# Half of the last layer norms moved from the attention's logits stage into the convolutions' logits stages, in a four-layer graph network

## The reference

```python
h = relu(_layernorm(x)); x = x + L0(h, edge_attr, ...)   # GINE: gather, sum, MLP, batch norm
h = relu(_layernorm(x)); x = x + L1(h, ...)              # two GATv2 convolutions, 4 heads
h = relu(_layernorm(x)); x = x + L2(h, ...)              # GAT with a small MLP
h = relu(_layernorm(x)); x = x + L3(h, edge_index)       # x + 0.5 * mean over the edges
```

## Time and profile before

| | us |
|---|---|
| median of 3 runs (range) | 4635.77 (4630.58 to 4641.23) |
| the profiled execution, its own time | 4636.25 |
| its span | 4634.5 |
| conv_logits of convolution 0, start to the next stage's start | 1549.5 to 2075.8 |
| conv_logits of convolution 1, first gathers to its last logit | 2437.8 to 2965.8 |
| gat_logits, start to the next stage's start | 3389.3 to 3714.7 |

### The profile page before, as it was taken

The page is one execution under the profiler, slowest core; times in us unless marked ns, Lnnn a source line. Parts: engine busy times, 40 slices in busy tenths (PEclk is TensorE's granted clock), DMA queues, the critical chain, the costliest instruction groups (busy, mean ns, idle before and its releaser), DMA issues. The chain is left out here.

```text
span 4634.5 us, 66260 instructions
## 1 busy us (share of the span) xinstructions
PE 3307.0 (71%) x15560; PEld 1990.1 (43%) x15560; DVE 3210.8 (69%) x10235; ACT 2604.3 (56%) x7608; POOL 2915.7 (63%) x2865
## 2 busy tenths in 40 slices
PE   2544288688888699985987999678856559973332
PEld 2444133477777334333663343245522235553331
DVE  2322299688888578876876888679978868863332
ACT  2322299588888577763774777446667725530000
POOL 6777677488887677756877875135577400037776
PEclk7766599899999899997998999889978879975555
DMA  8433388567776466656984545299979957653331
GB/s 327 117 98 87 120 282 279 179 239 243 238 243 216 152 213 209 215 171 199 327 269 135 166 157 163 79 311 334 328 257 346 325 143 230 225 174 98 98 96 53
DMA packets 549485, 942.99 MB, mean 203 GB/s; under 512 B 86253, under 2 KB 170248, under 8 KB 547204
## 3 DMA queue, kind: packets, MB, share of 16 engines
q1 hardware_dynamic: 481252, 800.20, 51.4%
q0 software_dynamic: 65856, 113.13, 9.2%
q10 hardware_dynamic: 2016, 25.69, 1.3%
HBM read 563.37 MB, written 381.14 MB: 204 GB/s over the span
## 5 line engine op out<-in xcount | busy, mean ns | idle before, releaser
L1163 DVE TENSOR_TENSOR conv_logits_leaky<-conv_logits_z,conv_logits_sloped 128x512 f32<-128x512 f32 x784 | 516.8, 687 | 111.7 <-ACT conv_logits_sloped L1097 103.1
L1097 ACT ACTIVATE conv_logits_sloped<-conv_logits_z 128x512 f32<-128x512 f32 x784 | 459.4, 596 | 176.3 <-PE conv_logits_z L1059 121.2
L1438 PE MATMUL conv_aggregate_part<-conv_aggregate_weighed,conv_wlc 128*128 128x512 f32 x784 | 360.1, 603 | 38.9 <-DVE conv_aggregate_weighed L1520 38.9
L1059 PE MATMUL conv_logits_z<-conv_logits_hdT,conv_logits_wsum 128*128 128x512 f32 x784 | 367.2, 612 | 15.1 <-DVE conv_logits_leaky L1163 13.1
L1066 PE MATMUL conv_logits_z<-conv_diffT,conv_logits_wl 128*128 128x512 f32 x784 | 352.9, 593 | 0.0
L748 PE MATMUL node_chain_o<-node_chain_ident,node_chain_biasT 128*128 128x128 f32 x784 | 220.5, 281 | 118.8 <-ACT node_chain_hT L844 117.2
L749 PE MATMUL node_chain_o<-node_chain_wmean,node_chain_hT 128*128 128x128 f32 x1568 | 273.8, 277 | 0.0
L1520 DVE TENSOR_TENSOR conv_aggregate_weighed<-conv_aggregate_alpha,conv_diffT 128x512 f32<-128x512 f32 x392 | 256.0, 713 | 10.0 <-DMA conv_aggregate_alpha<-ALPHA 10.0
L1930 PE MATMUL mean_edges_turned<-mean_edges_ident,mean_edges_hs 128*128 128x128 f32 x196 | 54.5, 434 | 278.0 <-DMA mean_edges_hs<-H,idx 278.0
L113 POOL DMA_INDIRECT gat_logits_hs<-H,idx x196 | 212.6, 1085 | 59.9 <-issue 58.0
L1972 DVE SCALAR_TENSOR_TENSOR mean_edges_rows<-mean_edges_back,mean_edges_half,mean_edges_base 128x128 f32<-128x128 f32 x196 | 55.3, 344 | 275.8 <-DMA out<-mean_edges_rows,idx 266.7
(11 more groups left out here) (297 smaller groups left out, 10609.0 us busy)
## 6 DMA issues: line engine op xcount, KB each, us to landing
conv_aggregate_alpha<-ALPHA SPq DMA_DIRECT2D x392, 256.0 KB, 5.2
HX<-node_chain_hx SPq DMA_DIRECT2D x98, 512.0 KB, 3.2
AGG<-gine_edges_zero ACTq DMA_DIRECT2D x14, 1792.0 KB, 36.1
gine_mlp_x<-x SPq DMA_DIRECT2D x98, 256.0 KB
gine_mlp_agg<-AGG SPq DMA_DIRECT2D x98, 256.0 KB
YT<-gine_mlp_yT SPq DMA_DIRECT2D x98, 256.0 KB, 4.4
node_chain_x<-x SPq DMA_DIRECT2D x98, 256.0 KB, 3.2
node_chain_yT<-YT SPq DMA_DIRECT2D x98, 256.0 KB, 2.7
```

The costliest lines, as they stand in the source:

```text
L1059: pe.matmul(z[h][:, :], wsum[:, h * D:(h + 1) * D], hdT[j % 3][:, :], start=True, stop=True).then_inc(z_done[0], 1)
L1097: act.activation(sloped[(H * (2 * j + c) + h) % S][:, :], z[h][:, :], ACT.Copy, scale=SLOPE).then_inc(sloped_made[c], 1)
L1163: dve.tensor_tensor(leaky[H * c + h][:, :], z[h][:, :], sloped[(H * (2 * j + c) + h) % S][:, :], ALU.max).then_inc(leaky_made[c], 1)
L1438: last = pe.matmul(part[n % 2][:, :], g.wlc[:, h * D:(h + 1) * D], weighed[n % 2][:, h, :], start=(h == 0), stop=(h == H - 1))
```

## The change

`ends_here(d)` is true for odd d. For the 24 odd dense tiles of each convolution the last norm and the result are made in `conv_logits`. `last_moments` and `last_scales` stand in DVE's turn d+3, `last_root` in ACT's turn d+3, `last_normalize` (writes `h4`, one buffer) in ACT's turn d+4; `last_sum` (`x2 + h4`) in turn d+4, on DVE in convolution 0 and on POOL in convolution 1; SP stores `H4` and `out` in turn d+5 and no longer stores `X3` for these tiles. The `x2` ring grows from 5 to 6. `gat_logits` keeps the 50 other dense tiles and takes an edge tile in every turn. The `sloped` ring is gone: ACT writes `sloped` into the `leaky` buffer, and DVE takes the maximum in place; `slope` now waits for the dots of the tile before in place of a maximum.

```diff
+def ends_here(d):
+    return d % 2 == 1
...
-    each, R, X, L, Q, S = 64 if spread else 128, 6 if spread else 5, 5, 3 if spread else 2, 2, 3
+    each, R, X, L, Q = 64 if spread else 128, 6 if spread else 5, 6, 3 if spread else 2, 2
...
+                def store_last(d):
+                    if ends_here(d):
+                        q = d // 2
+                        sp.wait_ge(h4_made, q + 1)
+                        sp.dma_start(node_rows(g.H4, node(d)), h4[:, :, :]).then_inc(h4_out, 16)
+                        sp.wait_ge(total_made, q + 1)
+                        sp.dma_start(node_rows(g.out, node(d)), x2[d % X][:, :, :]).then_inc(x3_out[d % X], 16)
-                sweep(N, [(0, load if spread else store_rows), (3, store_logits), (4, store_node), (0, load_x2)])
+                sweep(N, [(0, load if spread else store_rows), (3, store_logits), (4, store_node), (5, store_last), (0, load_x2)])
...
-                sweep(N, [(1 - R, fetch)] + ([(2, add_mlp_row)] if spread else []))
+                sweep(N, [(1 - R, fetch)] + ([(2, add_mlp_row), (4, last_sum)] if spread else []))
...
-                            turn_of, q = divmod(H * (2 * j + c) + h - S, H)
-                            past(act, leaky_made[turn_of % 2], H * (turn_of // 2) + q + 1)
-                            act.activation(sloped[(H * (2 * j + c) + h) % S][:, :], z[h][:, :], ACT.Copy, scale=SLOPE).then_inc(sloped_made[c], 1)
+                            if h == 0:
+                                past(act, dots_done[c], j)
+                            act.activation(leaky[H * c + h][:, :], z[h][:, :], ACT.Copy, scale=SLOPE).then_inc(sloped_made[c], 1)
...
-                sweep(N, [(1, slope(0)), (2, normalize), (2, copy_dots(1))] + ([] if spread else [(0, copy_dst)]) +
-                      [(0, lambda d: norm.root(act, d % X, d + 1, eps)), (1, slope(1)), (1, copy_dots(0))])
+                sweep(N, [(1, slope(0)), (2, normalize), (4, last_normalize), (2, copy_dots(1))] + ([] if spread else [(0, copy_dst)]) +
+                      [(0, lambda d: norm.root(act, d % X, d + 1, eps)), (3, last_root), (1, slope(1)), (1, copy_dots(0))])
...
+                sweep(N, [(1, leak(0)), (0, node_moments), (3, last_moments)] + ([(0, spread_dst)] if spread else []) + [(0, diff), (1, leak(1))] +
+                      [(1, lambda d: norm.scales(dve, d % X, d + 1)), (3, last_scales)] + ([] if spread else [(2, add_mlp_row), (4, last_sum)]))
...
 def gat_logits(nc, g):
-    N, M = g.NTE, g.NTN
+    N = g.NTE
+    left = [layer * N + d for layer in range(2) for d in range(N) if not ends_here(d)]
+    M = len(left)
...
-                    if t % 2 == 0:
-                        lane(t // 2, N, [(2, store_logit), (-2, load_dst)])
+                    lane(t, N, [(2, store_logit), (-2, load_dst)])
```

More of the change, by code:

```diff
@@ L923, in conv_logits @@
             hdx, hdx_out = m.sbs("hdx", [P, SUB, 2, D], n=R), m.sems("hdx_out", R)
-        sloped, leaky = m.sbs("sloped", [P, TILE], n=S), m.sbs("leaky", [P, TILE], n=2 * H)
+        leaky = m.sbs("leaky", [P, TILE], n=2 * H)
         logit = [m.sbs(f"logit{j}_", [P, TILE], n=L) for j in range(2)]
@@ L1028, in fetch, with last_sum @@
                         keep_place(j + 1)
-                sweep(N, [(1 - R, fetch)] + ([(2, add_mlp_row)] if spread else []))
+                def last_sum(d):
+                    if ends_here(d):
+                        wait_alone(pool, h4_made, d // 2 + 1, own)
+                        pool.tensor_tensor(flat(x2[d % X]), flat(x2[d % X]), flat(h4), ALU.add).then_inc(total_made, 1)
+                sweep(N, [(1 - R, fetch)] + ([(2, add_mlp_row), (4, last_sum)] if spread else []))
                 if spread:
@@ L1110, in normalize, with last_root, last_normalize @@
                     norm.apply(act, h3[d % Q], x2[d % X], d % X, ACT.Relu).then_inc(h3_made, 1)
+                def last_root(d):
+                    if ends_here(d):
+                        final.root(act, d // 2 % 3, d // 2 + 1, eps)
+                def last_normalize(d):
+                    if ends_here(d):
+                        q = d // 2
+                        act.wait_ge(final.shift_done, q + 1)
+                        past(act, h4_out, 16 * q)
+                        past(act, total_made, q)
+                        final.apply(act, h4, x2[d % X], q % 3, ACT.Relu).then_inc(h4_made, 1)
                 act.wait_ge(eps_set, 1)
-                sweep(N, [(1, slope(0)), (2, normalize), (2, copy_dots(1))] + ([] if spread else [(0, copy_dst)]) +
-                      [(0, lambda d: norm.root(act, d % X, d + 1, eps)), (1, slope(1)), (1, copy_dots(0))])
+                sweep(N, [(1, slope(0)), (2, normalize), (4, last_normalize), (2, copy_dots(1))] + ([] if spread else [(0, copy_dst)]) +
+                      [(0, lambda d: norm.root(act, d % X, d + 1, eps)), (3, last_root), (1, slope(1)), (1, copy_dots(0))])
             @block.vector
@@ L1160, in step @@
                             dve.wait_ge(sloped_made[c], H * j + h + 1)
[L1161 to L1164, removed]
+                            dve.tensor_tensor(leaky[H * c + h][:, :], z[h][:, :], leaky[H * c + h][:, :], ALU.max).then_inc(leaky_made[c], 1)
                     return step
@@ L1176, in add_mlp_row, with last_moments, last_scales, last_sum @@
                     last.then_inc(x3_made, 1)
-                sweep(N, [(1, leak(0)), (0, node_moments)] + ([(0, spread_dst)] if spread else []) + [(0, diff), (1, leak(1))] +
-                      [(1, lambda d: norm.scales(dve, d % X, d + 1))] + ([] if spread else [(2, add_mlp_row)]))
+                def last_moments(d):
+                    if ends_here(d):
+                        q = d // 2
+                        dve.wait_ge(x3_made, d + 1)
+                        past(dve, h4_made, q - 2)
+                        final.take_stats(dve, x2[d % X], q % 3)
+                        final.moments(dve, q % 3, q + 1)
+                def last_scales(d):
+                    if ends_here(d):
+                        final.scales(dve, d // 2 % 3, d // 2 + 1)
+                def last_sum(d):
+                    if ends_here(d):
+                        dve.wait_ge(h4_made, d // 2 + 1)
+                        dve.tensor_tensor(flat(x2[d % X]), flat(x2[d % X]), flat(h4), ALU.add).then_inc(total_made, 1)
+                sweep(N, [(1, leak(0)), (0, node_moments), (3, last_moments)] + ([(0, spread_dst)] if spread else []) + [(0, diff), (1, leak(1))] +
+                      [(1, lambda d: norm.scales(dve, d % X, d + 1)), (3, last_scales)] + ([] if spread else [(2, add_mlp_row), (4, last_sum)]))
 def edge_softmax(nc, g, layer, self_loops, share, spread=0):
```

23 lines of the change are left out of this document (13 added, 10 removed).

## The result

| | us |
|---|---|
| before, median of 4 runs (range) | 4637.5 (4630.6 to 4641.2) |
| the changed kernel, median of 4 runs (range) | 4691.3 (4676.4 to 4696.2) |
| ratio (95% interval) | 1.0114 (1.0096 to 1.0132) |
| conv_logits of convolution 0, start to next stage | 526.3, after 600.2 |
| conv_logits of convolution 1, start to next stage (with the softmax behind it) | 540.3 (581.7), after 558.6 (599.2) |

The changed kernel is 1.1% slower; 4629 was forecast, and at most 4662. The other stages moved by under 3 us each, together by -6: 74 + 18 - 30 - 6 are the 56 us between the two spans.

A forecast was written before the change was run, and what follows sets the result against it. It took gat_logits to be bound by full DMA engines and conv_logits0 by a full PE. From 4636.25 it added 29 (conv_logits0) and 16 (conv_logits1) and took off 52 (gat_logits): 4629 us, range 4602 to 4662.

The forecast's parts named there:

- conv_logits0, forecast 29: Added cost in conv_logits0: 28 us from late loads, 2 at the stage's end, 1 saved at its start; 29.
- The loop: conv_logits0: load of `x2` behind the `out` store, which waits for `last_sum`; round trip 21.45 us against 20.16 for two tiles.
- I take 3.4: conv_logits0: time from the load of `x2` to the moments, taken as 3.4 us, between 2.84 and 3.69.
- The estimate of 2.6: Load of `x2`: about 2.0 us fixed plus bytes over 436 GB/s; by it the kernel would take 4611.
- The rival with 4.3: conv_logits0: loads wait in DMA queues, 4.3 us to DVE; round trip 22.35, cost 49, kernel 4649; chance 0.22.
- gat_logits, forecast -52: gat_logits: 56 us gained by an earlier last copy to `srcT`, less 4 for slower gathers; gain 52.
- 1.257 for a gather: gat_logits: gathers speed up from 1.39 to 1.257 us each, as in conv_logits0, with DMA share at 0.76.
- the third rival: gat_logits: gathers stay at 1.39 us, from another cause than full DMA engines; gain 30, kernel 4651; chance 0.13.
- conv_logits1, forecast 16: Added cost in conv_logits1: 6 us in even turns, 8 once near its start, 2 at its end; 16.
- The 0.26 in each even turn: conv_logits1: second moments add 1.31 us against 1.05 spare, 0.26 in each of 22 even turns; 6 us.
- The 8 us at tile 6: conv_logits1: POOL late at the start, so tile 6's moments start at 2533.1 instead of 2525.10; 8 us, once.
- pairs over 22.5: conv_logits0: sign of being wrong; `z_self` pairs over 22.5 us apart, against 21.4 expected, would mean another wait in the loop.

The follow-up runs named there:

- x6: Changed kernel, conv_logits0's 512 KB store of gathered rows moved from directly behind the load of `x2` to behind the store of `X3`: 4703.1 us, 1.0144 of the kernel before.
- x5: Changed kernel plus two unread 128x512 matmuls ahead of `z_self` in conv_logits0's even turns from turn 6: 4666.9 us, 1.0067 of the kernel before.
- x12: Changed kernel with SP's load of `x2` ahead of the `H4` and `out` stores, and gat_logits' addition as four of 128x128: 4627.7 us, 0.9983 of the kernel before.
- x2: Changed kernel with gat_logits' addition made as four of 128x128, on the slower kind of chip: 4996.1 us, 0.9986 of the kernel before there.
- b2: Kernel before with only the `sloped` edit (shared `leaky` buffer), on the slower kind of chip: 5020.9 us, 1.0001 of the kernel before there.

## Why the prediction was wrong

- conv_logits0, forecast 29, measured 74. The loop was the right one, and every step but one has its size: 0.41 to the load, 4.36 from moments to `z_self` (forecast 4.39), 13.23 through the odd turn (13.25). The step that failed is "I take 3.4" for the load: 4.3. The trace of the kernel before had said so: the prediction calls 4.97 nearly the longest of the waits there, but six took longer, up to 5.43, and their median is 4.45. The estimate of 2.6 from the Trainium skill, DMA: Bandwidth & Descriptors, section Anatomy of one DMA, where the fit is for DMAs that GpSimd issues while SP issues this load, lies under every load that DVE waited for (2.75 to 6.68 in the changed kernel and x6). The rival with 4.3 gave 22.35 us a pair; 22.3 was seen. That is some 20 us. I had argued that the big store of the earlier trace rows no longer stood ahead; x6 shows that a distance from this store doesn't shorten the load.
- The second failure was a term that was missing. PE's idle 2 us cost more than themselves: 13 of the `z_self` behind them ran longer, up to 5.37, at a granted clock of 0.91 to 0.97 in the stretches of 50 us. x5 measured it, 19 us in the stage. 29 + 20 + 19 is 68, what x12 gave back, and 6 us are left, at the stage's start and end and in one wait, as x12 shows.
- gat_logits, forecast -52, measured -30. The step that failed is 1.257 for a gather because the DMA engines are no longer full (their share did fall to 0.76): the third rival was right, 1.39 each and a gain of 30. The excess came from the DVE addition. Fewer additions (50 for 98) did not help: 42 of the 50 each held a gather up, for 0.65 us in the mean, where 58 of the 98 had held one up for 0.45.
- conv_logits1, forecast 16, measured 18 in its stage. The 0.26 in each even turn were 0.24. The 8 us at tile 6 were 0.36, for POOL's `last_sum` was issued in time; in their place the first `last_moments` waited 4.22 for POOL's row, and PE 15.26 where it had waited 10.2. The size was right in part by luck.
- The sum's sign hung on two rivals at once, the tighter loop and the gathers. Together they give 4629 + 20 + 22 = 4671, beyond the range, which took them "in part together"; the clock's 19 bring it to 4690. Two of the prediction's own signs of being wrong came true: pairs over 22.5, and gat_logits less than 40 us shorter.

## What to carry to other kernels

A load that stands in a queue behind a store that waits for the end of a turn is a loop: move the load ahead of the store before counting whether the engines have room. Read a gather's excess by its coincidences: list the other engines' instructions beside the long ones, and see whether the ends, not the starts, keep a fixed distance. An idle gap ahead of matmuls can cost more than its length: here two us of it were often followed by 1.7 us more at a lower granted clock.

## What the hardware showed that was not expected

- In gat_logits an addition of 128x512 on DVE with both inputs in SBUF made a gather issued beside it end 0.82 us after the addition; the same with one input in PSUM did nothing to it. In the changed kernel an addition held the gather when it began up to 0.55 us into it, and no longer from 0.59 on. That is no general rule: in the kernel before, 16 additions that began 0.00 to 0.56 into a gather, each behind more than 1 us of idle time on DVE, left it at 0.94 to 0.95, while all 24 that began 0.06 to 0.07 into one straight behind another DVE instruction held it. The constant row's additions in conv_logits0, also from SBUF, coincided with 54 gathers and made 3 of them long, but `last_sum` there made 16 of 21 long (1.05 to 1.36). What separates the cases wasn't settled.
- Two matmuls that nobody reads, put in PE's wait, made the kernel 24 us faster.
- The sign of a change can hang on the chip: on B x2, the changed kernel but for its additions, was 0.14% faster than the kernel before. Against b2's trace, from another chip B, conv_logits0 took 12 us more there (680.5 for 668.4) and not 74, conv_logits1 15 us more, and gat_logits 44 less (318.4 for 362.0) and not 30. So the loop that lost the time on A cost little where conv_logits0 took 668 us already.
